# Plain attention: the row maxima, their transpose and the shift handled by halves of 512 queries, with the second half's maxima made inside the group itself

## What is computed

```python
qkv = jnp.einsum('bnd,ed->bne', z, W_qkv)
qkv = qkv.reshape(b, n, k, 3, Dh).transpose(3, 0, 2, 1, 4)
q, kk, v = (qkv[0], qkv[1], qkv[2])
scores = jnp.einsum('bhnd,bhmd->bhnm', q, kk) * scale
A = jax.nn.softmax(scores, axis=-1)
out = jnp.einsum('bhnm,bhmd->bhnd', A, v)
```

## Time and profile before

| | us |
|---|---|
| median of 3 runs | 1903.45 (1901.55 to 1904.09) |
| the profiled execution: its time | 1902.35 |
| the profiled execution: its span | 1900.5 |
| plain attention, first exp to last exp | 94.5 to 804.1 |
| mean granted TensorE clock, share of full | 0.96 |

### The profile page before, as it was taken

One profiled execution on the slowest core, in us unless ns is written; L12 is line 12 of the kernel. 1 busy time (PEld: TensorE's weight loads), 2 busy tenths in 40 slices (PEclk: granted clock), 3 DMA queues, 4 the chain that ended last, 5 costly groups with the idle time before them and its releaser, 6 DMA issues. The chain is left out here.

```text
span 1900.5 us, 33445 instructions
## 1 busy us (share of the span) xinstructions
PE 1642.3 (86%) x12948; PEld 626.3 (33%) x12948; DVE 1193.8 (63%) x2146; ACT 1441.7 (76%) x2508; POOL 269.1 (14%) x292
## 2 busy tenths in 40 slices
PE   5599999999999999854888898989889887883995
PEld 3122222222222222241333333433343332222773
DVE  7999999999999998586454536454645423223220
ACT  4188877777877788823999999999989999992321
POOL 4400000000000000032000100010001032212466
PEclk9699999999999999976999999999999999996998
DMA  5301111111111110004111211123111222331433
GB/s 168 98 13 55 46 43 38 38 44 38 38 38 43 38 38 22 2 31 140 45 45 55 88 63 51 51 72 96 51 47 62 85 83 91 96 117 56 126 56 30
DMA packets 69839, 115.85 MB, mean 61 GB/s; under 512 B 9689, under 2 KB 54597, under 8 KB 65072
## 3 DMA queue, kind: packets, MB, share of 16 engines
q1 hardware_dynamic: 58416, 92.87, 15.5%
q0 software_dynamic: 11264, 20.83, 4.0%
HBM read 71.49 MB, written 42.14 MB: 60 GB/s over the span
## 5 line engine op out<-in xcount | busy, mean ns | idle before, releaser
L768 ACT ACTIVATE rows_and_probs<-psS 128x512 f32<-128x512 f32 x999 | 543.5, 596 | 176.2 <-PE psS L666 174.5
L790 DVE TENSOR_REDUCE max_of_halves<-psM 128x2 f32<-128x1024 f32 x512 | 617.7, 1222 | 44.5 <-PE psM L630 15.1
L1616 ACT ACTIVATE exps<-cpsS 128x1024 bf16<-128x1024 f32 x512 | 544.1, 1099 | 26.6 <-PE cpsS L1358 24.2
L1358 PE MATMUL cpsS<-rotary_stack 128*128 128x512 bf16 x1024 | 302.8, 385 | 71.0 <-ACT exps L1616 27.1
L686 PE MATMUL psO<-rows_and_probs,plain_v 128*9 128x256 f32 x4096 | 316.9, 381 | 6.6 <-issue 2.3
L1626 ACT ACTIVATE cprobs<-cpsS 128x1024 f32<-128x1024 f32 x256 | 280.0, 1094 | 21.7 <-PE cpsO L1391 18.9
L1338 PE MATMUL cpsS<-rotary_stack 128*128 128x512 bf16 (+3 forms) x768 | 193.6, 329 | 54.4 <-ACT exps L1616 35.7
L630 PE MATMUL psM<-plain_top 64*128 64x512 bf16 x1024 | 209.9, 391 | 24.5 <-DVE max_of_halves L790 24.1
L666 PE MATMUL psS<-plain_top 64*128 64x512 bf16 x999 | 207.3, 388 | 6.5 <-issue 6.5
L666 PE MATMUL psS<-plain_rest 64*128 64x512 bf16 x999 | 202.0, 377 | 0.0
L1391 PE MATMUL cpsO<-cprobs,rotary_v 128*9 128x512 f32 (+3 forms) x1536 | 153.7, 488 | 0.8 <-DVE rotary_sums L1950 0.8
(11 more groups left out here) (300 smaller groups left out, 1705.5 us busy)
## 6 DMA issues: line engine op xcount, KB each, us to landing
rotary_stack<-q_parts SPq DMA_DIRECT2D x48, 192.0 KB
rotary_stack<-k_parts SPq DMA_DIRECT2D x48, 192.0 KB
rotary_stack<-q_rot_parts SPq DMA_DIRECT2D x48, 192.0 KB
rotary_stack<-k_rot_parts SPq DMA_DIRECT2D x48, 192.0 KB
tokens_taken<-parts_and_sums POOLq DMA_DIRECT2D x32, 259.0 KB, 4.0
plain_top<-q_parts SPq DMA_DIRECT2D x64, 96.0 KB
plain_top<-k_parts SPq DMA_DIRECT2D x64, 96.0 KB
e_x<-tokens_taken SPq DMA_DIRECT2D x8, 518.0 KB
```

The source lines that it names most:

```text
L768: act.activation(pr[n % SLOTS_P][:, h, :], score_bank(u), ACT.Exp, scale=SCALE).then_inc(s_e, 1)
L790: dve.tensor_reduce(mh[g % 2][:, :, hh, t, kh:kh + 1].rearrange("p e o -> p (e o)"), psM[n % 2][:, :, :], AX.X, ALU.max).then_inc(s_r, 1)
L1358: ins = pe.matmul(to[:, kh, :], q[:, x, y_ * P:(y_ + 1) * P], k[:, x, kh * CH:(kh + 1) * CH], start=True, stop=True)
L1616: act.activation(ex[d % EX][:, :, :], psS[n % 3][:, :, :], ACT.Exp, scale=SCALE, accum_out=den[:, at:at + 1]).then_inc(s_e, 1)
```

## The change

Everything that belongs to a maximum is cut into two halves by queries, cq = 0 and 1:

- A pair's number now counts the query half first (block_of), so the pairs 0 to 15 serve the queries 0 to 511 and the pairs 16 to 31 the others. max_of_halves and negated_max exist per query half; negation, turn, shift_parts and the 3 shift DMAs run twice per group, each for 16 rows instead of 32.
- plain_rest of q is laid out by query half, and its load takes 4 DMAs instead of 2 (6 per group with those of k).
- Before group 0 only the pairs 0 to 21 of group 0 are made, with the turn of its first half behind pair 16. In group g the slots 0 to 9 (two per half) carry the pairs 22 to 31 of the same group and the slots 10 to 31 the pairs 0 to 21 of group g+1. The turn of the second half stands at the start of half 6, that of the next group's first half at the start of half 14. The wait on s_sh stands at half 0 and at half 8, each for its own query half.
- Group 15 now has 10 pairs and one turn, and its scores go over 5 banks from half 7 on. first_rows and fw.quantise both stand behind that turn, and so behind the merge of group 14 and ahead of the merge of group 15.
- SP: the loads of group 1 and of the tops of group 2 now come behind the first shift of group 0. In each group the order is: shift of the first half, wait for the scores of the group before, loads, shift of the second half.

```diff
-        return range(SHARE * (ci - FIRST_BLOCK), SHARE * (ci - FIRST_BLOCK + 1) if ci < NCH - 1 else PAIRS)
+        return range(SHARE * (ci - FIRST_BLOCK), SHARE * (ci - FIRST_BLOCK + 1) if ci < NCH - 1 else PAIRS // 2)
+    TURN_AT = (14, 6)
+    def pair_behind(g, slot):
+        ahead = slot - (PAIRS // 2 - LEAD)
+        g, m = (g, PAIRS + ahead) if ahead < 0 else (g + 1, ahead)
+        return (g, m) if g < G else None
+    order = [("pair", 0, m) for m in range(PAIRS // 2 + 1)] + [("turn", 0, 0)]
+    order += [("pair", 0, m) for m in range(PAIRS // 2 + 1, PAIRS // 2 + LEAD)]
+    for g in range(G):
+        for slot in range(2 * HALVES):
+            if slot == 2 * MERGE_AT + 1 and g:
+                order.append(("merge", g - 1, 0))
+            if slot == 2 * TURN_AT[1]:
+                order.append(("turn", g, 1))
+            if slot == 2 * TURN_AT[0] and g + 1 < G:
+                order.append(("turn", g + 1, 0))
+            if pair_behind(g, slot):
+                order.append(("pair",) + pair_behind(g, slot))
...
-        LAST, spare = (G - 1) * UNITS, psM[use["merge", G - 1, 0] % 2]
+        LAST, spare = (G - 1) * UNITS + (TURN_AT[1] + 1) * HG, psM[use["merge", G - 1, 0] % 2]
...
             def exp_group(g):
-                pe.wait_ge(s_sh, (g + 1) * (16 * PARTS))
                 for half in range(HALVES):
+                    if half == TURN_AT[1]:
+                        max_turn(g, 1)
+                    if half == TURN_AT[0] and g + 1 < G:
+                        max_turn(g + 1, 0)
+                    if half % TB == 0:
+                        pe.wait_ge(s_sh, (2 * g + half // TB + 1) * (16 * PARTS))
                     two_scores(g, half, 0)
...
-                    if half == 14 and g + 1 < G:
-                        max_turn(g + 1)
...
-            tops_of(1)
-            for m in range(1):
-                max_pair(1, m)
-            max_turn(0)
-            for m in range(1, LEAD):
-                max_pair(1, m)
+            max_pair(0, PAIRS // 2)
+            max_turn(0, 0)
+            for m in range(PAIRS // 2 + 1, PAIRS // 2 + LEAD):
+                max_pair(0, m)
...
-                    shift_parts(g)
-                    if g == G - 1:
-                        dve.wait_ge(s_mg, 2 * (G - 2))
+                    shift_parts(g, m)
+                    if g == G - 1 and m:
                         first_steps = first_rows()
+                        dve.wait_ge(s_fr, first_steps)
+                        fw.quantise(dve)
                 else:
                     merge(g)
-                    if g == G - 2:
-                        dve.wait_ge(s_fr, first_steps)
-                        fw.quantise(dve)
...
             project.sync(sp, x, w_qkv, w_gate, w_up, w_down)
-            stacks.load_tops(sp, 1)
-            stacks.load_rests(sp, 1)
-            stacks.load_tops(sp, 2)
             for g in range(G):
-                sp.wait_ge(s_shp, g * 3 + 3)
-                for j in range(PARTS):
-                    sp.dma_start(xq[g % 2][SHIFT_AT + j::P // 2, :, :].rearrange("o h (t n) -> o (h t) n", t=TB),
-                                 shp[:, j, :]).then_inc(s_sh, 16)
+                store_shift(g, 0)
                 if g:
                     sp.wait_ge(s_s, g * UNITS)
-                    if g + 1 < G:
-                        stacks.load_rests(sp, g + 1)
-                    if g + 2 < G:
-                        stacks.load_tops(sp, g + 2)
+                else:
+                    stacks.load_tops(sp, 1)
+                if g + 1 < G:
+                    stacks.load_rests(sp, g + 1)
+                if g + 2 < G:
+                    stacks.load_tops(sp, g + 2)
+                store_shift(g, 1)
```

More of the change, by code:

```diff
@@ L452, in rest_copies @@
                 at = e * (P // 2)
-                todo.append((self.rest[n][g % 2][at:at + DH, :, :].rearrange("r h n -> r (h n)"),
-                             rows[PARTS - 1, g, e, :, :, :].rearrange("d h n -> d (h n)")))
+                if n:
+                    todo.append((self.rest[n][g % 2][at:at + DH, :, :].rearrange("r h n -> r (h n)"),
+                                 rows[PARTS - 1, g, e, :, :, :].rearrange("d h n -> d (h n)")))
+                else:
+                    todo += [(self.rest[n][g % 2][at:at + DH, cq, :, :], rows[PARTS - 1, g, e, :, :, cq * CH:(cq + 1) * CH])
+                             for cq in range(2)]
         return todo
@@ L576, in softmax_phase @@
         pr = [arena[:, i * HG * CH:(i + 1) * HG * CH].rearrange("p (h n) -> p h n", h=HG) for i in range(SLOTS_P)]
[L577 to L580, removed]
+        mh = [[sb(f"max_of_halves{i}_{cq}", [P, 2, HG // 2, TC, 2]) for cq in range(2)] for i in range(2)]
+        nm = [sb(f"negated_max{cq}", [P, HG * TC]) for cq in range(2)]
+        ra = sb("rest_of_max", [HG * TC, P])
+        shp = sb("shift_parts", [HG * TC, PARTS, P], BF16)
         rd = sb("rden", [P, TB * HG])
@@ L665, in two_scores @@
                         rows, hh = rows_of(h // (HG // 2)), h % (HG // 2)
+                        queries = q[rows, cq, hh, :] if part else q[rows, hh, cq * CH:(cq + 1) * CH]
                         ins = pe.matmul(score_bank(u), k[rows, hh, j * P:(j + 1) * P],
-                                        q[rows, hh, cq * CH:(cq + 1) * CH], start=(part == 0), stop=(part == 1),
+                                        queries, start=(part == 0), stop=(part == 1),
                                         skip_group_check=True)
@@ L720, in next_pair @@
             def next_pair(g, half, n):
[L721 to L724, removed]
+                todo = pair_behind(g, 2 * half + n)
+                if todo:
+                    if todo[1] == 0:
+                        tops_of(todo[0])
+                    max_pair(*todo)
             def pairs_between(ci):
@@ L858, in _ @@
             project.vector(dve, pairs_between)
-            for kind, g, m in order[PAIRS:]:
+            for kind, g, m in order[PAIRS // 2:]:
                 if kind == "pair":
```

74 lines of the change are left out of this document (35 added, 39 removed).

## The result

The changed kernel takes 1895.76 us (median of 5 runs, 1894.16 to 1897.10) against 1903.45 (5 runs, 1901.55 to 1904.09): 7.7 us less, ratio 0.9959, 95% interval 0.9947 to 0.9972. In a second measurement on another occasion the ratio was 0.9965 (0.9953 to 0.9977). The profiled execution took 1896.76 us, its span is 1895.0.

What follows compares the result with a forecast made beforehand. DVE was taken to bound the stretch before group 0, PE the groups. Terms -18.1, +2.7, +0.7, +1.7 and +1.1 sum to -11.9 us, against the median of 1903.45 giving 1891.5 us; range 1885 to 1898.5.

Steps and rivals of the forecast that it cites:

- Step 1: Ahead of group 0: 16 pair reductions fewer on DVE, first exp from 94.47 to 76.4, -18.1 us.
- C: Start held by something other than DVE, such as SP's loads; half of the 18.1 lost, 1900 us; chance 0.05.
- Step 2: Groups 0 to 13: boundary stalls go, -7.0, but each group gets a second turn; +2.7 us in all.
- The margin of 0.84 us: At the wait on s_sh: 5.68 us from the transpose to cover the shift's chain of 4.84 us.
- Rival D: Slower: second shift lands late in every group behind 18 loads; at 2.5 us of delay 1906 us; chance 0.03.
- Steps 3 to 5: Group 14 +0.7 us, group 15 +1.7 us, DVE's work at the end +1.1 us.
- step 5: End of group 15: first_rows and quantise keep DVE busy, so the last merge comes 1.1 us late.
- Rival A: Turns are free: DVE not in PE's way mid-group, a middle turn costs 0.28; 1885.8 us; chance 0.14.
- B: Turns cost more: DVE's backlog does not drain, each middle turn costs 1.1 us; 1896.5 us; chance 0.15.
- E: Group 0 starts sooner, but the maxima of its second half make the first group DVE-bound; chance 0.01.
- The estimate of 10 us a group: In each group: five added DMAs, if each paid a fixed 2.0 us in a row, cost 10 us.

## Why the prediction was right, and where it was not

The forecast was 1891.5 us, 11.9 below; it came out 7.7 below in the medians and 6.3 below at the last merge of the two traces. The sign and the range were right, the size was between half and two thirds of the forecast.

| step | forecast | by the traces |
|---|---|---|
| 1, start | -18.1 | -13.7 |
| 2, groups 0 to 13 | +2.7 | +3.8 |
| 3 and 4, groups 14 and 15 | +2.4 | +2.3 |
| 5, DVE at the end | +1.1 | +1.2 |
| sum to the last merge | -11.9 | -6.3 |

**Step 1 failed in one sentence:** "the tail from turn to first exp is as before". The 16 reductions did go, 1.13 us each, and no wait on loads took their place; SP's issue of the loads ran from 77.7 to 97.0 and PE didn't wait for them. But by coming 18 us sooner the turn moved into a stretch in which GpSimd was still at work, and there its cast was held for 4.0 us. GpSimd's share of this stretch stood in the rows that the forecast rested on: 15.10 us busy of 20. The prediction doesn't mention GpSimd, and says of this stretch that nothing else is due in it. The remaining 0.4 to 0.5 is DVE's start of the ten reductions (58.12 instead of 57.64), which varies from run to run. The rival that came closest was C, the start held by something else than DVE; it looked for SP and the shift's queue, and the cause was a third engine's claim on what DVE shares with it. It had been given 0.05.

**Step 2** was right in each mechanism and short in size. The stalls at the boundaries are gone. The middle turn costs 0.65 us instead of 0.60 in a plain group. With statistics DVE's backlog holds PE one slot earlier too: the quarter ahead of the turn and the turn's own take 279.08 - 274.09 = 4.99 us together in group 4, where the kernel before took 290.77 - 286.96 = 3.81 without a turn, so 1.18 instead of 1.10. From merge to merge the plain groups are 0.14 longer (44.54 to 44.68) where 0.10 was expected, those with statistics 0.68 (45.67 to 46.35) where 0.60 was. That gives 1.4 and 2.0 for ten and three; the rest is one of the plain groups, longer by 0.39 instead of 0.14, and 0.1 in group 0. Moving the merge brought back 4.9 of the expected 5.0 and shows that it is DVE's backlog.

**The margin of 0.84 us** for the shift at half 8 was about right: with one half less of cover the stall is 1.66, so the change has 2 x 1.32 - 1.66 = 1.0 in hand. Rival D, the slow one, was not near. But its price was worked out wrongly: at 2.5 us of delay the stall is 2.5 - 0.84 = 1.66, 16 of them are 26.6, and the sum is +14.7, or 1918 us and not 1906. The run with the turn in half 7 had just this stall and was 22.9 us slower than the changed kernel up to the merge of group 15, its turn being further from the merge.

**Steps 3 to 5** came out as forecast. From the merge of group 13 to the first scores of group 15 it is 0.7 us longer (755.12 - 723.64 = 31.48, before 764.27 - 733.52 = 30.75), from there to the last exp 1.6 (41.41 against 39.80). That step 5 is quantise's place was tested by leaving it out: 1.05 of the 1.22 us went. The change's own gain in groups 14 and 15 was read rightly too: pairs in the idle time of group 14 cost nothing.

**Rival A** (turns free), **B** (1.1 us in each plain group, where 0.65 was measured) and **E** fell.

The estimate of 10 us a group from the Trainium skill ("DMA: Bandwidth & Descriptors", section "Anatomy of one DMA"), for five more DMAs in a group, didn't come true: the plain groups are 0.14 us longer. That section gives its fixed part for DMAs issued by GpSimd, and these are issued by SP; the prediction didn't say so.

## What to carry to other kernels

When work is taken out ahead of a chain, read what every other engine does at the hour to which the chain moves, GpSimd too, and ask of each instruction in the chain what it shares with it: here a 0.2 us cast became one of 4.2, and either a wait of one line or another form of the instruction gave it back. The smallest and longest time of one line, beside each other, find such a hold in the trace before anything is changed: 333 and 1304 ns at L304. A step whose cost is set by a backlog belongs several slots away from the other steps that make one; moving the merge away from the turn brought 4.9 us. Spare time of 0.19 us a slot is not a place for pieces of 0.95, even if the sum fits.

## What the runs showed of the hardware

- A cast from SBUF to SBUF on DVE waits for GpSimd's memsets; subtractions with one operand from PSUM, or with two from SBUF, do not (0.28 us beside them, 4.22 for the cast), nor does the cast that reads PSUM (0.27).
- A tensor_scalar from SBUF to SBUF waits for GpSimd's subtractions (1.19 to 1.30 us instead of 0.34, in the kernel before). The profile shows such a wait as a long busy time of the DVE instruction, not as idle time ahead of it.
- The wait usually ends at the next boundary between memsets (0.42 to 1.55 us in four runs) but in the changed kernel lasted 4.0 us, over three boundaries, five times out of five. Why is open.
- The untouched phases behind the step vary by 7 us from trace to trace (1088.6 to 1095.8), and the point in time at which DVE starts its last stretch before group 0 by 2.5 us (55.60 to 58.15). Differences below some 3 us had to be read inside the trace.
